# First self attention of a two-layer perceiver block: query and value projections as three split products, key projection in fp32 with its low-rank part last, low-rank products side by side

## The reference

```python
def lora_linear(x, W, b, Bm, Am):                      # RANK 16, SCALING 0.5
    out = jnp.einsum('bld,od->blo', x, W) + b
    upd = jnp.einsum('blr,or->blo', jnp.einsum('bld,rd->blr', x, Bm), Am)
    return out + SCALING * upd
q = _split(lora_linear(x, Wq, bq, Bq, Aq))             # x is the layer-normed residual
k = _split(lora_linear(x, Wk, bk, Bk, Ak))
v = _split(lora_linear(x, Wv, bv, Bv, Av))             # 16 heads of 32
attn = jax.nn.softmax(jnp.einsum('bhqd,bhkd->bhqk', q, k) * SCALE, axis=-1)
out = jnp.einsum('bhqk,bhkd->bhqd', attn, v)           # heads merged again
return lora_linear(out, Wo, bo, Bo, Ao)
```

## Time and profile before

| | us |
|---|---|
| median of 3 runs | 1483.12 (1482.01 to 1488.65) |
| the profiled execution's own time | 1493.27 |
| its span, first to last instruction | 1491.5 |
| mean granted share of TensorE's full clock | 0.957 |
| PE busy / DVE busy / ACT busy / POOL busy | 1390.7 / 1006.9 / 778.2 / 78.4 |

### The profile page before, as it was taken

How to read it: one execution, slowest core, us unless ns; L and a number is a source line. 1 busy time by engine, 2 the same in 40 slices (tenths; PEclk the granted TensorE clock), 3 DMA queues, 4 the chain that set the end, 5 groups by cost and what they waited for, 6 DMA issues and landing times. The chain is left out here.

```text
span 1491.5 us, 31870 instructions
## 1 busy us (share of the span) xinstructions
PE 1390.7 (93%) x11742; PEld 1074.0 (72%) x11742; DVE 1006.9 (68%) x1659; ACT 778.2 (52%) x1134; POOL 78.4 (5%) x71
## 2 busy tenths in 40 slices
PE   6999999999969889999989999969999588999998
PEld 4677776777735489999977877846666355899997
DVE  7666676666636467666547777768999644676664
ACT  3777777777732455454432322327888113455542
POOL 0000000000011300000011111110000100000000
PEclk9999999999989989999999999978999669899999
DMA  5443544333232087656125332237775111676662
GB/s 162 86 92 91 124 104 86 85 84 84 50 113 105 1 266 267 211 181 213 36 58 183 107 130 100 84 89 167 170 170 128 55 43 56 204 232 215 212 210 74
DMA packets 133599, 191.20 MB, mean 128 GB/s; under 512 B 74987, under 2 KB 96717, under 8 KB 130317
## 3 DMA queue, kind: packets, MB, share of 16 engines
q1 hardware_dynamic: 133533, 190.30, 44.3%
HBM read 154.12 MB, written 17.48 MB: 115 GB/s over the span
## 5 line engine op out<-in xcount | busy, mean ns | idle before, releaser
L187 PE MATMUL psum<-m_x_hi,m_gu_hi 128*128 128x256 f32 x780 | 223.1, 286 | 2.1 <-DVE m_h L2404 1.8
L188 PE MATMUL psum<-m_x_hi,m_gu_lo 128*128 128x256 f32 x780 | 222.6, 285 | 0.0
L189 PE MATMUL psum<-m_x_lo,m_gu_hi 128*128 128x256 f32 x780 | 222.5, 285 | 0.0
L1544 DVE TENSOR_REDUCE x_peaks<-psum 128x2048 f32 (+1 forms) x64 | 146.3, 2291 | 50.4 <-PE psum L1422 50.4
L187 PEld LDWEIGHTS psum<-m_x_hi,m_gu_hi 128*128 128x128 f32 x780 | 151.1, 194 | 5.7 <-DVE m_h L2404 2.2
L188 PEld LDWEIGHTS psum<-m_x_hi,m_gu_lo 128*128 128x128 f32 x780 | 151.0, 194 | 1.5
L187 PE MATMUL psum<-x_w_hi,x_ctx_hi 128*128 128x256 f32 x512 | 151.9, 297 | 0.0
L189 PEld LDWEIGHTS psum<-m_x_lo,m_gu_hi 128*128 128x128 f32 x780 | 151.0, 194 | 0.0
L504 ACT ACTIVATE x_probs<-psum 128x1024 f32<-128x1024 f32 x128 | 124.1, 1022 | 45.9 <-PE psum L394 45.8
L504 ACT ACTIVATE x_w_raw<-psum 128x1024 f32<-128x1024 f32 x128 | 124.2, 1025 | 41.3 <-PE psum L394 37.3
L188 PE MATMUL psum<-x_w_hi,x_ctx_lo 128*128 128x256 f32 x512 | 144.9, 283 | 0.0
(11 more groups left out here) (319 smaller groups left out, 2826.3 us busy)
## 6 DMA issues: line engine op xcount, KB each, us to landing
m_gu_raw<-in_m_gu SPq DMA_DIRECT2D x41, 768.0 KB, 4.3
e_w<-x_keys_dram SPq DMA_DIRECT2D x45, 512.0 KB, 6.8
m_gu_raw<-in_m_gu SPq DMA_DIRECT2D x18, 1024.0 KB, 4.9
x_ctx_raw<-in_ctxT SPq DMA_DIRECT2D x64, 256.0 KB, 2.8
m_dn_raw<-in_m_down SPq DMA_DIRECT2D x16, 768.0 KB, 4.3
m_dn_raw<-in_m_down SPq DMA_DIRECT2D x18, 512.0 KB, 5.2
x_keys_dram<-x_keys_hi SPq DMA_DIRECT2D x16, 512.0 KB, 3.2
x_keys_dram<-e_wqp SPq DMA_DIRECT2D x16, 512.0 KB, 2.7
```

What stands on the lines that cost most here:

```text
L187: pe.matmul(out, a[0], b[0], start=start, stop=False, skip_group_check=True)
L188: pe.matmul(out, a[1], b[0], start=False, stop=False, skip_group_check=True)
L189: return pe.matmul(out, a[0], b[1], start=False, stop=stop, skip_group_check=True)
L1544: dve.tensor_reduce(peaks[:, t, 4 * m:4 * m + 4, bass.ds(k, 1)].rearrange("p h k -> p (h k)"), g.psum[:, at:at + BANKS, :], AX, ALU.max).t ...
```

## The change

Per part:

1. The down products of q, k and v become one group of 4 matmuls with 96 stationary columns. Each 16-row factor is laid out in 32 columns (repeated), so the result has q, k, v at partitions 0, 32 and 64 of one bank. `low` and `up` have the same layout (96 rows); the output projection's up weights get a tensor of their own, `up_o`.
2. The key projection stays fp32, but only its first up product waits for `low`, after the first four main matmuls.
3. The query and value projections become `product3` on fp32r halves of the input and the weights. ACT makes the rounded halves, DVE the remainders.
4. ACT instead of DVE rounds the key/value weights of the second cross attention; POOL does two of the four subtractions, DVE the other two.
5. Wo is loaded into Wk's buffer, so its load waits for `k_done`. `up_o` is loaded behind it.

The core of the diff:

```diff
-        w = [sb("w" + n, [P, NC, D], F32) for n in names]
-        down = sb("down", [P, NC, 4, RANK], F32)
-        up = sb("up", [RANK + 1, 4, D], F32)
-        low = sb("low", [RANK + 1, 4, L], F32)
+        w = [sb("w" + n, [P, NC, D], F32) for n in names[:3]]
+        w.append(w[1])
+        down = sb("down", [P, NC, 4, 2 * RANK], F32)
+        up = sb("up", [3 * 32, D], F32)
+        up_o = sb("up_o", [RANK + 1, D], F32)
+        low = sb("low", [3 * 32, L], F32)
...
+                    sp.wait_ge(k_done, 1)
+                    load_weight(sp, 3)
+                    sp.dma_start(up_o[:, :], A["a0_up_o"]).then_inc(up_o_loaded, 16)
...
+                    for c in range(NC // 2):
+                        pool.wait_ge(kv_rounded, c + 1)
+                        pool.tensor_tensor(g.x1_w_lo[:, c, :], kv_raw[:, c, :], g.x1_w_hi[:, c, :].bitcast(F32),
+                                           ALU.subtract)
...
+                    for c in range(NC):
+                        last = pe.matmul(g.bank[0][0:3 * 32, 0:L], down[:, c, 0:3, :].rearrange("p n r -> p (n r)"),
+                                         g.xnT[:, c, :], start=(c == 0), stop=(c == NC - 1))
...
                     for m in range(NC):
-                        o = g.bank[4 + 2 * n + m // 2][:, (m % 2) * L:(m % 2 + 1) * L]
+                        o = g.bank[6 + m // 2][:, (m % 2) * L:(m % 2 + 1) * L]
                         for c in range(NC):
-                            pe.matmul(o, w[n][:, c, m * P:(m + 1) * P], g.xnT[:, c, :], start=(c == 0), stop=False)
-                        last = pe.matmul(o, up[:, n, m * P:(m + 1) * P], low[:, n, :], start=False, stop=True)
+                            pe.matmul(o, w[1][:, c, m * P:(m + 1) * P], g.xnT[:, c, :], start=(c == 0), stop=False,
+                                      skip_group_check=True)
+                        if m == 0:
+                            pe.wait_ge(lowo_made, 3)
+                        last = pe.matmul(o, up[low_rows(1), m * P:(m + 1) * P], low[low_rows(1), :], start=False,
+                                         stop=True, skip_group_check=True)
+                    last.then_inc(k_done, 1)
+                    pe.wait_ge(x_split, 1)
+                    for m in range(NC):
+                        o = g.bank[4 + m // 2][:, (m % 2) * L:(m % 2 + 1) * L]
+                        pe.matmul(o, up[low_rows(0), m * P:(m + 1) * P], low[low_rows(0), :], start=True, stop=False,
+                                  skip_group_check=True)
+                        for c in range(NC):
+                            if m == 0:
+                                pe.wait_ge(w_split, c + 1)
+                            last = product3(pe, o, halves(0, (c, slice(m * P, (m + 1) * P))),
+                                            [b[:, c, :] for b in (x_hi, x_lo)], False, c == NC - 1)
+                    last.then_inc(q_done, 1)
+                    for t in range(NT):
+                        for c in range(NC):
+                            if t == 0:
+                                pe.wait_ge(w_split, NC + c + 1)
+                            product3(pe, g.bank[2 + t][:, :], [b[:, c, t * P:(t + 1) * P] for b in (x_hi, x_lo)],
+                                     halves(1, (c, slice(0, D))), c == 0, False)
+                        last = pe.matmul(g.bank[2 + t][:, :], low[low_rows(2), t * P:(t + 1) * P], up[low_rows(2), :],
+                                         start=False, stop=True, skip_group_check=True)
+                    last.then_inc(v_done, 1)
...
+                    act.activation(x_hi[:, :, :], g.xnT[:, :, :], ACT.Copy).then_inc(x_rounded, 1)
+                    round_w(0)
+                    round_w(1)
+                    act.wait_ge(q_done, 1)
...
+                        act.wait_ge(kv_loaded[c], 16)
+                        act.activation(g.x1_w_hi[:, c, :], kv_raw[:, c, :], ACT.Copy).then_inc(kv_rounded, 1)
+                    act.wait_ge(v_done, 1)
```

More of the change, by code:

```diff
@@ L858, in stage_attn0 @@
         stage_layernorm(nc, g, "ln_a0_", prefetch)
[L859 to L880, removed]
-                    for c in range(NC):
[L882 to L888, removed]
@@ L895, in _ @@
-                pe.wait_ge(w_loaded[2], 16)
-                for t in range(NT):
-                    for c in range(NC):
[L898 to L904, removed]
@@ new lines, in _, with split_w @@
+                    last.then_inc(v_done, 1)
+                @block.vector
+                def _(dve):
+                    def split_w(i):
+                        for c in range(NC):
+                            dve.wait_ge(w_rounded, NC * i + c + 1)
+                            dve.tensor_tensor(w_lo[:, i, c, :], w[SPLIT[i]][:, c, :],
+                                              w_hi[:, i, c, :].bitcast(F32), ALU.subtract).then_inc(w_split, 1)
+                    dve.wait_ge(low_cleared, 1)
+                    dve.wait_ge(low_made, 1)
+                    for n in range(3):
+                        rows = slice(32 * n, 32 * n + RANK)
+                        dve.tensor_scalar(low[rows, :], g.bank[0][rows, 0:L], LORA, None,
+                                          ALU.mult).then_inc(lowo_made, 1)
+                    dve.wait_ge(x_rounded, 1)
+                    dve.tensor_tensor(x_lo[:, :, :], g.xnT[:, :, :], x_hi[:, :, :].bitcast(F32),
+                                      ALU.subtract).then_inc(x_split, 1)
+                    split_w(0)
+                    split_w(1)
+                    dve.wait_ge(k_done, 1)
+                    dve.wait_ge(pad_cleared, 1)
+                    pad = k_pad[:, :, :].rearrange("p (m j) n -> p m j n", j=4)
+                    for j in range(4):
+                        for b in range(2):
+                            dve.tensor_copy(pad[32 * j:32 * j + 32, 2 * b:2 * b + 2, j, :],
+                                            g.bank[6 + b][32 * j:32 * j + 32, :].rearrange("p (m n) -> p m n", m=2))
+                    for s in range(2):
+                        dve.wait_ge(ctx_loaded[s], 16)
+                        dve.tensor_copy(g.x1_ctx_hi[:, s, :, :], ctx_raw[:, s, :, :]).then_inc(ctx_rounded, 1)
+                        dve.wait_ge(ctx_rounded, s + 1)
+                        dve.tensor_tensor(g.x1_ctx_lo[:, s, :, :], ctx_raw[:, s, :, :],
+                                          g.x1_ctx_hi[:, s, :, :].bitcast(F32), ALU.subtract)
+                    for c in range(NC // 2, NC):
+                        dve.wait_ge(kv_rounded, c + 1)
+                        dve.tensor_tensor(g.x1_w_lo[:, c, :], kv_raw[:, c, :], g.x1_w_hi[:, c, :].bitcast(F32),
+                                          ALU.subtract)
@@ L957, in _ @@
                 for c in range(NC):
-                    last = pe.matmul(g.bank[0][0:RANK, 0:L], down[:, c, 3, :], outT[:, c, :],
+                    last = pe.matmul(g.bank[0][0:RANK, 0:L], down[:, c, 3, 0:RANK], outT[:, c, :],
                                      start=(c == 0), stop=(c == NC - 1))
@@ L965, in _ @@
                                   start=(c == 0), stop=False)
+                    pe.wait_ge(up_o_loaded, 16)
                     pe.wait_ge(low2_made, 1)
[L967 removed]
+                    pe.matmul(g.bank[2 + t][:, :], low[low_rows(0), t * P:(t + 1) * P], up_o[:, :],
                               start=False, stop=True).then_inc(out_done, 1)
```

89 lines of the change are left out of this document (48 added, 41 removed).

## The result

| | runs | median (lowest to highest), us | ratio to the kernel before, 95% interval |
|---|---|---|---|
| kernel before, same chip | 20 | 1487.33 (1481.80 to 1490.84) | |
| changed kernel | 20 | 1482.82 (1478.54 to 1484.62) | 0.9969 (0.9959 to 0.9978) |

The change makes the kernel 0.31% faster. The interval leaves no doubt about the sign, but the gain is about half of the forecast's 0.59%, and the time, 1482.82 us, lies above the forecast's range (1469 to 1481). The three runs of before that were shown ahead (1483.12) lay 4.2 us under the median of these 20. The profiled execution of after has a time of 1483.47 and a span of 1481.6 us.

The account below looks back on a forecast made before the run. PE was taken to bound the projection block, busy wall to wall except one hole. Terms -6.05 + 1.05 - 1.96 - 1.8 gave -8.8 us, a factor 0.9941, so 1474.3 us from the median 1483.1; range 1469 to 1481.

Parts of the forecast that it names:

- key product's start: Projection block: key product starts at 438.35 instead of 444.40, with no wait for Wk or `low`; -6.05 us.
- key at half clock: Key product: its first 2.45 us run at half clock until 440.8, so it takes 11.25 instead of 10.20; +1.05 us.
- query: Query product: four slices of 2.06 us, with 12 fp32r matmuls each, take 8.24 instead of 10.20; -1.96 us.
- value, with the end: Value product: two tiles of 3.77 us take 7.5 (+0.1 for the last result) instead of 9.4; -1.8 us.
- Down products and Wk: Block's start: 8 down-product records take 3.4 us, ending at 438.3; Wk, no longer behind one slow engine, lands about then.
- Wk as late as before: Rival, chance 0.10: PE idles from 438.3 to 442.5 waiting for Wk; gain 5.6 us, or 3.0 with a slow clock.
- slow-clock branch: Late-Wk case: clock rises 6.0 us after PE's restart, sum -3.0, 1480.1 us; with clock up at once, -5.6, 1477.5 us.
- Halves: Rounded halves and remainders of input and weights are ready before PE asks, hidden behind the key product; no stall.
- All end before PE's 465.4: Block's end: DVE, ACT and POOL side work is done before PE, POOL's subtractions at 464.8, DVE's near 464.4.
- POOL ends last: Rival, chance 0.10: POOL and DVE subtractions exclude each other, taking 7.2 us until 467.2; price 0.7 us, 1475.0 us.
- the one from the block to the whole: After the block: core, output projection and later stages have the same instructions, so the block's -8.8 us reaches the total.
- rival of half-clock stretches: Rival, chance 0.15: later half-clock stretches grow; one growing by 3.4 us leaves a 7.1 us gain, 1476.0; two leave 5.4.

Follow-up runs that it names:

- e_up17: Changed kernel with only `up` loaded as three pieces of 17 rows instead of one of 96; ratio 1.0000 to the kernel before, block 39.03 us.
- g_ups: Changed kernel with all query and value up products in one row behind the key's last, every slice keeping its low-rank part; ratio 0.9967 to the kernel before.
- e_start: Changed kernel with query and value projections left in fp32 and no halves made for them; ratio 0.9965 to the kernel before, 0.9973 in a repeat.
- f_fill_moe: Changed kernel plus products of zeros on PE, 11 ahead of and 6 into the first mixture's start; ratio 0.9986 to the kernel before.
- f_ups: Changed kernel with all query and value up products in a row behind the key's last, query's low-rank part lost in every other slice; 0.9962 to the kernel before.

## Why the prediction was wrong, by its own steps

**The sum over the block was right in this pair of profiles: -8.54 us against -8.8.** The profile after against that of before, term by term:

| term | forecast | measured | from |
|---|---|---|---|
| key product's start | -6.05 | -5.72 | 9.56 to 3.84 us after the block's start |
| key at half clock | +1.05 | +0.52 | 438.95 to 449.67: 10.72 instead of 10.20 |
| query | -1.96 | -1.91 | 449.67 to 457.96: 8.29 instead of 10.20 |
| value, with the end | -1.8 | -1.43 | 457.96 to 467.34: 9.38 instead of 10.81 |

*Down products and Wk.* 3.70 us and +3.84 against 3.4 and +3.5; no engine left alone with `up`. `e_up17` shows that this was the cause: rival "Wk as late as before" is what happens without the 96-row load, and its slow-clock branch, not its fast one. It was even too mild: it had -3.0 us for the block, `e_up17` has -1.7.

*Key.* A mean clock of 0.56 over the window 434.80 to 440.80 says that it rose some 0.7 us earlier than I had it, so the half-clock part cost half.

*Query.* Right by two misses that cancel. A slice takes 2.25 us (451.30 to 453.55), not 2.06: the step from the last main product to the up product (451.08 to 451.30) and the first step behind it (451.92 to 452.14) take 0.22 us instead of the pace of 0.12. The switch between fp32 and fp32r isn't needed for that. The kernel before has the same two steps with fp32 on both sides (read in narrow windows, so that single records show):

```profile
446.62 0.37 PE L893 MATMUL psum<-a_low,a_up 17*128 17x256 f32 x1
446.92 0.48 PE L892 MATMUL psum<-x_norm_T,a_wk 128*128 128x256 f32 x1
447.24 0.59 PE L892 MATMUL psum<-x_norm_T,a_wk 128*128 128x256 f32 x2
447.45 0.59 PE L892 MATMUL psum<-x_norm_T,a_wk 128*128 128x256 f32 x2
...
448.53 0.38 PE L892 MATMUL psum<-x_norm_T,a_wk 128*128 128x256 f32 x1
448.84 0.48 PE L893 MATMUL psum<-a_low,a_up 17*128 17x256 f32 x1
```

There 446.92 to 447.24 and 448.53 to 448.84 take 0.32 and 0.31 us, and 447.24 to 447.45, like the steps behind it, 0.21. What all these places share is the change between 128 and 17 rows. The sum took 12 equal steps for the main part and so left out 0.2 us that a slice had before as well. But the query's first up product runs beside the key's last: the four records at 449.05 and 449.37 take 0.63 us together, as long as one pair alone at 441.40 (0.62).

*Value.* The same steps are 0.3 of the missing 0.4 us: 460.49 to 460.81, 461.86 to 462.19 and 464.48 to 464.80 take 0.32 to 0.33 us instead of 0.23.

*Halves.* PE waited for none of them.

*POOL and DVE at the end.* "All end before PE's 465.4" failed. POOL's two take 2.84 us each instead of 2.39, DVE's two 2.46 instead of 1.23. From 460.27 to 467.04 the four take 6.77 us; the rival "POOL ends last" had 7.2, until 467.2. It was right that the two engines hinder each other, with the wrong engine last, and its price is nearly zero only since ACT's copy ends at the same moment. With PE faster (`g_ups`) it is the limit: without it the block is 1.1 and 1.9 us shorter. The Trainium skill, "SBUF — State Buffer", section "SBUF: two separate sides", gave this lock; the runs agree that the two hinder each other, though in 6.77 us and not quite one after the other.

**The step that failed is the one from the block to the whole.** "The attention core, the output projection and the later stages have the same instructions", and so the same time: they don't take it. The core takes 34.83 instead of 33.35 us, since the clock falls to 0.50 for 3.4 us as it starts. That gives back 1.48 of the 8.54 us, and nearly as much in the two repeats. What brings the fall is not shown. It is the rival of half-clock stretches (0.15, gain 7.1), as a new stretch rather than a grown one, and it fits: 8.54 - 1.48 = 7.1. The Trainium skill, "TensorE: Matmul & The Clock Gate", section "What's actually happening", has the window free-running, so that moved work can meet it differently; that this stretch comes and goes between kernels with the same core, and between two executions of `e_start`'s kernel, agrees.

**And the baseline was drawn high and low at once.** The block of the profiled execution was 0.66 us longer than the other profile of before, which leaves 8.54 - 1.48 - 0.66 = 6.4 us. With `f_fill_moe`'s profile counted in, block and core give 6.8 us on average. Measured are 5.7 in the mean spans (standard error 0.45) and 4.5 in the medians of the 20. The second cross attention, the second self attention and the second mixture differ between profiles of one kernel by 1 to 6 us, more than is left to explain, so the rest can't be placed. The median of three, 1483.12, to which I applied the ratio, was 4.2 us under the median of twenty. Of the 8.5 us between 1474.3 and 1482.8, about half is this and half the smaller gain.

## What to carry to other kernels

When a block ends, list the last instruction of every engine, not only the one of the engine that is longest: here PE could end 2.9 us earlier and the next stage came only 0.55 us earlier, until DVE's subtractions were freed from POOL's, and giving two of the four to POOL made DVE's share longer (4.92 us) than all four alone (4.63). A load in 17 rows ahead of a large one in the same queue delays the large one, and a wait of 3 us on PE may cost more than itself (here the 17 rows cost 4.9 us in the mean spans and 6.8 in the profiled block), since the clock stayed down behind it. Before a gain under 1% is forecast, measure the baseline with more than three executions (here its median moved by 4.2 us), and profile one kernel twice before a slow stretch is put down to an edit. Of what the block's profile showed, 67% arrived here.

## What I had not expected of the hardware

- Up products on different partitions of the array's input (0 to 16 and 32 to 48) run side by side: 0.63 us for two that take 0.62 each alone. With the up products in one row (`f_ups`, 448.52 to 451.40) five of 0.62 and two of 1.05 take 2.88 us instead of 5.2.
- The 24 records of down products take 5.67 and 5.89 us with results on partitions 0, 32 and 64, against 8.27 and 7.61 with all results on the partitions from 0. That they overlap too is only a guess.
- Next to an up product of 17 rows, a step between matmuls takes 0.1 us more than the pace, whether both are fp32 or one is fp32r: 0.32 instead of 0.21 us before, 0.22 instead of 0.12 in the split products.
- DVE beside POOL, both subtracting two operands in SBUF: 2.46 instead of 1.16 to 1.23 us for DVE, 2.84 instead of 2.39 for POOL.
- A 3.4 us stretch at half clock at a stage's start costs 1.5 us, and it comes and goes between executions of one and the same kernel.
